# Attention of a graph network on one core: moving VectorE's products, reductions and additions, and two kinds of TensorE products, in the written order of an iteration

## The reference, cut to what matters

```python
scores = jnp.sum(q_dst * kt, axis=-1) / scale        # per edge and head
m = jax.ops.segment_max(scores, dst, num_segments=N)  # largest of each target
e = jnp.exp(scores - m[dst])
s = jax.ops.segment_sum(e, dst, num_segments=N)
agg = jax.ops.segment_sum(V[src] * w[..., None], dst, num_segments=N)
```

## Time and profile before

| | |
|---|---|
| median of 3 timed runs | 5547.93 us (5539.17 to 5548.32) |
| span of the profiled execution | 6456.7 us; no time beside the span is given for that execution |
| busy in the span | PE 4457.4, DVE 3832.0, POOL 3364.1, ACT 1605.5 us |
| granted clock of TensorE, mean of the span | 0.831 |
| the four calls of `attend` in that span | 847, 846, 849 and 824 us |

### The profile page before, as it was taken

How to read it: one execution, slowest core, us unless ns; L and a number is a source line. 1 busy time by engine, 2 the same in 40 slices (tenths; PEclk the granted TensorE clock), 3 DMA queues, 4 the chain that set the end, 5 groups by cost and what they waited for, 6 DMA issues and landing times. The chain is left out here.

```text
span 6456.7 us, 68859 instructions
## 1 busy us (share of the span) xinstructions
PE 4457.4 (69%) x19341; PEld 3493.0 (54%) x19341; DVE 3832.0 (59%) x8692; ACT 1605.5 (25%) x3882; POOL 3364.1 (52%) x3108
## 2 busy tenths in 40 slices
PE   5666664577766666778857767796766679766776
PEld 4455453444436455557845555685555558545554
DVE  7544443544455666675347766643766776567777
ACT  3433332200004111113421211243211214312221
POOL 2588886366644555541356555134555530256663
PEclk9888887788888778779977777898778779878887
DMA  3688887255556555542266556315556541256664
GB/s 139 121 124 125 121 125 150 81 184 184 182 165 208 168 173 181 181 144 58 81 189 182 174 175 181 89 56 165 169 175 182 176 147 39 80 168 183 195 192 134
DMA packets 508435, 959.75 MB, mean 149 GB/s; under 512 B 85846, under 2 KB 298020, under 8 KB 507251
## 3 DMA queue, kind: packets, MB, share of 16 engines
q0 software_dynamic: 224512, 549.90, 34.1%
q1 hardware_dynamic: 283426, 404.92, 19.6%
q10 hardware_dynamic: 128, 0.52, 0.0%
HBM read 718.56 MB, written 236.50 MB: 148 GB/s over the span
## 5 line engine op out<-in xcount | busy, mean ns | idle before, releaser
L1460 POOL DMA_INDIRECT L2a_rows<-kv_rows,typed_index x960 | 966.3, 1007 | 627.8 <-DVE L2a_weighted L1615 349.9
L1765 PE MATMUL L2a_sums<-L2a_weighted,L2a_hot 128*128 128x264 f32 x2784 | 830.5, 450 | 166.8 <-DVE L2a_weighted L1615 159.4
L1754 PE MATMUL L2a_query<-x,L2a_turned 128*128 x2784 | 819.8, 447 | 55.8 <-ACT L2a_turned L1709 33.0
L867 POOL DMA_INDIRECT sum_rows<-L0s_rows,L0s_row_of x464 | 724.6, 1562 | 152.9 <-issue 119.4
L1765 PEld LDWEIGHTS L2a_sums<-L2a_weighted,L2a_hot 128*128 128x128 f32 x2784 | 591.2, 221 | 314.5 <-DVE L2a_weighted L1615 186.2
L1754 PEld LDWEIGHTS L2a_query<-x,L2a_turned 128*128 128x128 f32 x2784 | 627.2, 229 | 181.4 <-issue 62.5
L1460 POOL DMA_INDIRECT hold<-kv_rows,typed_index x432 | 445.4, 1031 | 449.8 <-DVE L2a_weighted L1615 279.5
L1460 POOL DMA_INDIRECT L3a_rows<-feature_rows,index x464 | 489.1, 1054 | 301.7 <-DVE L3a_weighted L1615 155.1
L1285 POOL DMA_INDIRECT L1s_rows<-rows,index x464 | 451.0, 972 | 351.2 <-issue 133.8
L1717 ACT ACTIVATE L2a_hot<-L2a_hot 128x512 f32<-128x512 uint8 x348 | 218.7, 629 | 1470.8 <-PE L2a_sums L1765 726.6
L1002 PE MATMUL L0s_message<-features,L0s_share 128*128 x928 | 312.8, 496 | 285.9 <-ACT L0s_share L967 285.9
(11 more groups left out here) (428 smaller groups left out, 8550.9 us busy)
## 6 DMA issues: line engine op xcount, KB each, us to landing
code_rows<-L1s_code SPq DMA_DIRECT2D x116, 512.0 KB
L3a_code<-code_rows SPq DMA_DIRECT2D x116, 512.0 KB
L0s_wide<-source_rows SPq DMA_DIRECT2D x116, 256.0 KB
L2a_turn<-turned_rows SPq DMA_DIRECT2D x87, 256.0 KB
L2a_pens<-mask_rows SPq DMA_DIRECT2D x87, 256.0 KB
L2a_hot<-hot_rows SPq DMA_DIRECT2D x87, 256.0 KB
kv_rows<-L2d_key_rows SPq DMA_DIRECT2D x50, 384.0 KB, 2.6
kv_rows<-L2d_value_rows SPq DMA_DIRECT2D x150, 128.0 KB, 2.4
```

The lines of the kernel that those rows point to most:

```text
L867: pool.indirect_dma_start(c.sum_rows[u], bass.IndirectOffsetOnAxis(ap=row_of[:, 4 * n + u:4 * n + u + 1], axis=0), rows[n % ring][:, u, :] ...
L1460: pool.indirect_dma_start(rows[n % ring][:, u, :], None, table, bass.IndirectOffsetOnAxis(ap=index_of[:, t:t + 1], axis=0)).then_inc(lande ...
L1754: last = pe.matmul(query[q % 2][:, u, :], turned[quad % 2][:, u, :], at(c.q, b[2 * q + u // 2]), start=True, stop=True)
L1765: last = pe.matmul(sums[(m * WP + j) % held][:, :], hot[quad % 2][:, j % 2 * 2 + k, :], weighted[:, 2 * j + k, :], start=k == 0, stop=k == 1)
```

## The change

No instruction is added or taken away. On DVE `reduce(n, 0)` goes behind `spread_ends`; `reduce(n, 1)` goes ahead of `chain_up`; `product(n, 2)`, an addition and `reduce(n, 2)` go ahead of `pick_own`; `product(n, 3)` goes ahead of `weigh(m, 0)` and `reduce(n, 3)` ahead of `weigh(m, 2)`. On PE `ask(n, 3)` goes ahead of `expand`, and `flatten(n)` ahead of `ask(n + 1, 1)`.

```diff
                 if chain:
                     scan_down(m)
+                if tail:
+                    add(m - 1, 4, before[4])
+                if chain:
+                    spread_ends(m)
                 if more:
                     reduce(n, 0)
-                if chain:
-                    spread_ends(m)
-                if tail:
-                    add(m - 1, 4, before[4])
-                if more:
+                    product(n, 1)
                     join(n, 0)
-                    product(n, 1)
...
                 if chain:
+                    grow(m)
+                if more:
+                    product(n, 2)
+                if tail:
+                    add(m - 1, 7, before[7])
+                if more:
+                    reduce(n, 2)
+                    join(n, 2)
+                if chain:
                     pick_own(m)
...
                     lower(m)
                 if more:
-                    product(n, 2)
-                if tail:
-                    add(m - 1, 7, before[7])
+                    product(n, 3)
                 if chain:
                     weigh(m, 0)
                     rescale(m, now[0])
-                if more:
-                    reduce(n, 2)
-                if chain:
                     weigh(m, 1)
                     add(m, 0, now[0])
                 if more:
-                    product(n, 3)
-                    join(n, 2)
+                    reduce(n, 3)
                 if chain:
                     weigh(m, 2)
...
                 if more:
                     ask(n, 2, now)
+                    ask(n, 3, now)
                 if chain:
                     expand(m)
-                if more:
-                    ask(n, 3, now)
-                if chain:
                     unflatten(m)
...
+                if more:
+                    flatten(n)
                 if ahead:
                     ask(n + 1, 1, near)
-                if more:
-                    flatten(n)
```

More of the change, by code:

```diff
@@ L1643, in _ @@
                     scan_down(m)
+                if tail:
+                    add(m - 1, 4, before[4])
+                if chain:
+                    spread_ends(m)
                 if more:
                     reduce(n, 0)
-                if chain:
-                    spread_ends(m)
-                if tail:
-                    add(m - 1, 4, before[4])
-                if more:
+                    product(n, 1)
                     join(n, 0)
-                    product(n, 1)
-                if chain:
-                    chain_up(m)
                 if tail:
                     add(m - 1, 5, before[5])
-                if chain:
-                    chain_down(m)
                 if more:
@@ L1661, in _ @@
                 if chain:
-                    grow(m)
+                    chain_up(m)
+                if more:
+                    join(n, 1)
+                if chain:
+                    chain_down(m)
                 if tail:
@@ L1665, in _ @@
                 if chain:
+                    grow(m)
[6 more added lines that the diff above has]
+                    join(n, 2)
+                if chain:
                     pick_own(m)
-                if more:
-                    join(n, 1)
-                if chain:
                     join_own(m)
@@ L1693, in _ @@
                 if more:
-                    reduce(n, 3)
                     join(n, 3)
```

## The result

The changed kernel takes 5703.07 us (median of 4 runs, 5701.5 to 5709.85), the kernel before 5548.12 beside it (4 runs, 5539.17 to 5562.49): a ratio of 1.0281, 95% interval 1.0264 to 1.0298, 155 us slower. The forecast, 5805, had the sign, and was 102 us too far.

A forecast was written before the change was run, and what follows sets the result against it. POOL's fetch pace, about 20 us a group, was taken to bound the kernel; the ring would grow to 22.5 us. Over 112 passes, 2.1 to 2.5 us each make 235 to 280: 5548 + 257 = 5805 us, range 5470 to 5940.

The forecast's parts named there:

- the waits of the earlier trace: DVE idle for 772 us ahead of chain_up and pick_own in the profile; claimed nearly all absent from timed runs.
- POOL sets the pass before: In the attentions before the change, POOL's 16 fetches at 1.25 us hold a group to about 20 us.
- the ring: total(m, 0) to ask(n, 2) on PE, DVE to weigh, next total: 17.8 us before, 19.9 after, at full clock.
- The faster rival: The waits are real and the change fills them: a group falls from some 20.9 to 20.0 us, 5450 us; chance 0.22.
- The ring after: The ring with the work ahead of pick_own: 15.4 + 7.1 = 22.5 us at a clock of 0.83.
- The ring before: The unchanged ring, PE 12.8 plus DVE 5.0: 17.8 us at full clock, under POOL's 20.0.
- the prediction's three bounds: Per attention group: DVE's own work 19.2 us, POOL's 16 fetches 20.0, and the ring through PE, 17.8 at full clock.
- The other moves at nothing: Moves outside the priced ring, including reduce(n, 0), flatten and product(n, 3): at most 0 to 1 us a group lost.
- POOL hides it: At full clock the changed ring, 19.9 us, stays under POOL's 20.0: unchanged at 5548 us; chance 0.10.
- the clock falls further: PE's clock at 0.79 or less, plus 0.5 us for a waiting addition: 23.8 us a group, 5950 us; chance 0.13.
- Real waits: DVE's waits ahead of chain_up and pick_own are in timed runs and the change fills them: 5450 us; chance 0.22.
- The other sign: PE idle longer than 1.75 us ahead of the first total, mostly ended by DVE, would show the forecast right.

The follow-up runs named there:

- e1: The kernel before, unchanged, recorded a second time: 5544.58 us in its one run, span 5542.9 us.
- e9: The kernel before with the fourth fetch of each quad left out from the eleventh quad of a call on: 5397.85 us, ratio 0.9728.
- e10: The changed kernel with the fourth fetch of each quad left out from the eleventh quad of a call on: 5702.66 us, ratio 1.0295.
- e3: The kernel before with only the second half of DVE's new order, from product(n, 2), an addition and reduce(n, 2) ahead of pick_own on: 5703.48 us, ratio 1.0281.
- e8: As e3, but product(n, 3) too stands ahead of pick_own, and reduce(n, 3) behind lower: 5869.65 us, ratio 1.0576.
- e5: The kernel before with only the first half of DVE's new order, between spread_ends and chain_up: 5540.56 us, ratio 0.9989.
- e12: The kernel before with only flatten(n) moved ahead of ask(n + 1, 1) on PE: 5548.96 us, ratio 1.0004.
- e2: The kernel before with all of DVE's new order and PE's old order: 5701.9 us, ratio 1.0284.
- e6: The kernel before with only expand(m) moved behind ask(n, 3) on PE: 5596.81 us, ratio 1.0086.

## Why the prediction was right, and where it was off

**That the waits of the earlier trace rows aren't in the timed runs** was right: e1 has 6 us of the 772. That recording as such causes them was not: every kernel here was recorded, and the span of each lies within 0.3% of the median of its timed runs. Nor does the difference lie between timed runs without recording and a recorded one, as the text ahead of the prediction has it: the timed runs of the kernel before beside the experiments list a span and a granted clock too, the span 1.6 to 1.8 us under the time, so something is recorded of each. The waits belong to that one execution, and what made it 909 us longer stays open. The rule cited for it from the Trainium skill's "NOTIFIC — the notification-queue block", "7.1 Overflow: three behaviours, one of which stalls the engine", no run here shows.

**That POOL sets the pass before** was right (e9, e10). **Its size is the step that failed**: "POOL, which starts a fetch every 0.95 + 0.30 = 1.25 us even where nothing holds it up, so 16 take 20.0". The earlier trace rows is the shortest kind of fetch; the group's mean is 1.01 us in e1, and it stood at 1007, 1054 and 1031 ns in the first trace too. The pass is 20.8 to 21.4, 21.0 in the mean of the four calls, and not 20.0 to 20.4; against the middle of the two, 20.2, that is 0.8 us more cover for the ring, and over 112 passes some 90 us of the 102 by which the forecast overshot. The pass after, 22.4 in the mean against 22.5, gives the rest. The faster rival had worked out 20.9 for a middle pass, from a program 100 us shorter elsewhere; that number was right, its cause (waits worth filling) was not.

**The ring after**, 22.5 us, came out in its sum: 22.2 measured in L2a, 22.9 in L3a. e3 shows that it is the product, the addition and the reduction ahead of `pick_own`, e8 that 1.14 more lengthen it again. But its terms differ, and that they cancel is luck. In the mean of L2a's middle passes the trace has:

| stretch | predicted | measured, us |
|---|---|---|
| first total to the end of `ask(n, 2)` | 15.6 | 15.1 |
| to the start of `product(n, 2)` | 0 | 0.5 |
| to `pick_own` | 2.6 | 2.6 |
| to the end of `lower` | 1.5 | 1.5 |
| to `weigh` | 1.5 | 1.2 |
| to the next first total | 1.3 | 1.3 |

The clock was 0.87 and 0.85, not 0.83, which shortens the first stretch. The 0.5 us are no wait for PE: in the timeline above `ask(n, 2)`, the first half of the row at 2323.50, is done by about 2325.4, and DVE goes without a pause from `grow` (L1579, 2325.79) to `product(n, 2)` at 2325.92. So at that place DVE's own queue comes last, not `ask(n, 2)`: it has worked almost without a pause since the addition behind `scan_down`, which waits for PE's sums (2320.79, 0.16 us in the mean), and goes on so to `weigh`. The ring thus closes through DVE's first half too; the path that the prediction priced is shorter by some 0.5 us (0.3 in e3). DVE's additions (L1544) wait 129.6 us for sums in L2a, mostly behind `weigh`; what those waits cost was not tried.

**The ring before**, 17.8 us at full clock, is 12.8 / 0.91 + 5.0 = 19.1 at e1's clock. e9, with POOL out of the way, takes 19.3 in L2a, and DVE idles for only 0.14 us of such a pass (both in the median). So DVE's own work, one of the prediction's three bounds, sets e9's pass, and of the ring it shows only that it is not longer.

**The other moves at nothing**: right for the first half of DVE's order (e5) and for `flatten` (e12), both tried in the kernel before, where POOL's pace covers them; in the changed order e2, with the first half, and e3, without it, take the same time. `expand` behind `ask(n, 3)` is hidden only under the work ahead of `pick_own`; without that cover it costs 48 us (e6).

**The rivals.** "POOL hides it" fails by e10, "the clock falls further" by the windows, 0.87 and 0.85. "Real waits" fails by e1. Of what was to show the forecast right, the vanished wait with slower timed runs is there. The other sign, PE idle for longer than 1.75 us ahead of the first total, is not: that stand is 1.75 us after the change and was 1.96 before it (e1), 154.8 us against 212.2 over L2a's totals. The stand that grew lies ahead of `unflatten`, 218.9 us against 43.1, and was not named as a sign.

## What to carry to other kernels

A wait in a trace is worth filling only if the trace's time is that of the timed runs; where it isn't, record the kernel again first. Take a resource's pace from the mean of its group, not from one row: the difference between them was a contention here, and removing it (one operand in PSUM, 96 us) was worth more than any order tried. Work put between a request and its taking is free only up to the slack of the ring through both engines: at least 1.5 us here; beyond 2.6 us, 1.14 us more cost 1.1 to 1.7. And where both engines are nearly without pause, look which one comes last at each hand-over: a sum over one path can come out near by luck.

## What the runs showed of the hardware that was not expected

A `weigh` with both inputs in SBUF holds up a fetch that starts within it to 0.82 us behind its end, up to 2.0 us instead of 0.95; a fetch that runs already when `weigh` starts is not held up, and doesn't hold up `weigh`. One recorded execution in which takers start 4.5 to 5.9 us behind the end of small products has a span 914 us longer than the same program's next, 6456.7 against 5542.9 us.
